# Node updates around the attention layer of a graph network: three blocks in flight, inverse roots and row loads on GpSimd

## The reference

```python
edge_index = jnp.stack([src, dst])
x = _layernorm(x + _L0_gnn_ref(x, edge_attr_3, edge_attr_64, ..., edge_index), axis=-1)
x = _layernorm(x + _L1_gnn_ref(x, edge_attr_16, edge_attr_4, ..., edge_index), axis=-1)
x = _layernorm(x + _L2_gnn_ref(x, edge_index, edge_attr_4, node_vec1, ...), axis=-1)
x = _layernorm(x + _L3_gnn_ref(x, edge_index, edge_attr_4, node_vec1, ...), axis=-1)
```

```python
# layer 0, after the sum over edges
out_s = agg_s @ W_out_s + skip_s
out_v = jnp.einsum('nmi,mk->nki', agg_v, W_out_v) + skip_v
fs = jax.nn.silu(out_s[:, :MUL0])
gate = jax.nn.sigmoid(out_s[:, MUL0:MUL0 + 32])
gv = gate[:, :, None] * out_v
# layer 1, before the edges: s_n, v_n = _equiv_layernorm(s, v, ...), then two products by node
mu = jnp.mean(s, axis=-1, keepdims=True)
var = jnp.var(s, axis=-1, keepdims=True)
s_n = (s - mu) * jax.lax.rsqrt(var + EPS) * gamma_s + beta_s
rms = jnp.sqrt(jnp.mean(jnp.sum(v * v, axis=-1), axis=-1, keepdims=True) + EPS)
v_n = v / rms[..., None] * gamma_v[None, :, None]
# layer 1, after the edges: softmax over the edges of a node, then
agg = jax.ops.segment_sum(alpha * h, dst, num_segments=n)
out = node + jnp.concatenate([agg_s @ Wps, ...], axis=-1)
# each layer norm
return (x - m) / jnp.sqrt(v + eps)
```

## Time and profile before

| | us |
|---|---|
| median of 3 runs | 26809.61 |
| lowest and highest | 26806.86, 26810.96 |
| the profiled execution | 26817.98 |
| its span, from the first instruction to the last | 26815.9 |
| n1, by its loads and stores | about 6185 to 6883 |
| n2 | about 17982 to 18533 |
| n3 and n4 | about 20930 to 22600 and 25070 to 26815 |

### The profile page before, as it was taken

The page is one execution under the profiler, slowest core; times in us unless marked ns, Lnnn a source line. Parts: engine busy times, 40 slices in busy tenths (PEclk is TensorE's granted clock), DMA queues, the critical chain, the costliest instruction groups (busy, mean ns, idle before and its releaser), DMA issues. The chain is left out here.

```text
span 26815.9 us, 474867 instructions
## 1 busy us (share of the span) xinstructions
PE 20099.6 (75%) x102170; PEld 15503.3 (58%) x102170; DVE 19989.9 (75%) x70096; ACT 11977.1 (45%) x39978; POOL 12176.7 (45%) x11987
## 2 busy tenths in 40 slices
PE   1566566664798898888988988973777787777788
PEld 1223222223677777777777777762555676555677
DVE  8333688883688888888888888876777666777666
ACT  0233344443566666666666666653333222333222
POOL 2777655551344444444444444432777101777200
PEclk6677788887788888888888888876999898999888
DMA  0566555553222222222222222222222100222200
GB/s 32 149 172 172 125 111 111 109 110 87 78 73 73 73 73 73 73 73 73 73 73 73 73 73 73 73 69 65 61 61 61 18 5 20 61 60 60 28 5 5
DMA packets 1781692, 1962.59 MB, mean 73 GB/s; under 512 B 754160, under 2 KB 1457344, under 8 KB 1780992
## 3 DMA queue, kind: packets, MB, share of 16 engines
q0 software_dynamic: 565056, 1310.16, 18.5%
q1 hardware_dynamic: 1216576, 651.75, 10.6%
HBM read 1399.54 MB, written 561.06 MB: 73 GB/s over the span
## 5 line engine op out<-in xcount | busy, mean ns | idle before, releaser
L1445 PE MATMUL e_sums<-e_feat,e_same 128*128 128x272 f32 x13824 | 3442.0, 403 | 1360.1 <-ACT e_feat L1466 1237.2
L1427 POOL DMA_INDIRECT e_rows<-x,e_take x3456 | 3618.9, 1047 | 1122.6 <-issue 1045.8
L977 POOL DMA_INDIRECT e_srow<-src_table,e_take x1620 | 1557.5, 961 | 5316.6 <-issue 5126.8
L1445 PEld LDWEIGHTS e_sums<-e_feat,e_same 128*128 128x128 f32 x13824 | 2594.4, 192 | 2207.4 <-issue 1596.4
L581 PE MATMUL e_sums<-e_feat,e_same 128*128 128x480 f32 x3456 | 1965.0, 724 | 1331.1 <-DVE e_feat L649 1331.1
L1012 PE MATMUL e_ps_m<-ident,e_m 128*128 128x128 f32 x12960 | 2333.4, 308 | 554.7 <-DVE e_m L1208 411.2
L565 POOL DMA_INDIRECT e_rows<-table,e_take x1728 | 1876.6, 1086 | 1381.0 <-issue 1351.6
L1012 PEld LDWEIGHTS e_ps_m<-ident,e_m 128*128 128x128 f32 x12960 | 1592.8, 159 | 1240.0 <-DVE e_m L1208 764.5
L581 PEld LDWEIGHTS e_sums<-e_feat,e_same 128*128 128x128 f32 x3456 | 801.9, 244 | 2494.1 <-issue 2407.6
L1026 PEld LDWEIGHTS e_ps_x<-ident,e_lg 128*128 128x128 f32 x12960 | 2188.0, 238 | 76.3
L1026 PE MATMUL e_ps_x<-ident,e_lg 128*128 128x128 f32 x12960 | 2143.5, 321 | 0.0
(11 more groups left out here) (306 smaller groups left out, 52898.4 us busy)
## 6 DMA issues: line engine op xcount, KB each, us to landing
e_pay<-pay_rows SPq DMA_DIRECT2D x432, 470.0 KB, 3.8
order_keys<-key_row SPq DMA_DIRECT2D x810, 128.0 KB
e_keys<-key_row SPq DMA_DIRECT2D x1620, 64.0 KB, 2.8
e_rows<-x,e_take POOLq DMA_INDIRECT x3456, 2.6
order_feat<-in_attr_T SPq DMA_DIRECT2D x810, 64.0 KB
comb<-n_comb SPq DMA_DIRECT2D x300, 164.0 KB, 1.9
e_rows<-table,e_take POOLq DMA_INDIRECT x1728, 4.1
pay_rows<-order_stage,order_put POOLq DMA_INDIRECT x1620
```

The source lines that it names most:

```text
L977: pool.indirect_dma_start(out=srow[t.j][:, :], out_offset=None, in_=src_table, in_offset=bass.IndirectOffsetOnAxis(ap=takes[0][t.j][:, :], ...
L1427: pool.indirect_dma_start(out=rows[t.j][:, q, :], out_offset=None, in_=x, in_offset=bass.IndirectOffsetOnAxis(ap=take[t.j][:, q:q + 1], ax ...
L1445: ins = pe.matmul(sums[b][q // G][:, 512 * h:512 * h + HALF], same[b][:, q, :], feat[b][:, q, h * HALF:(h + 1) * HALF], start=q % G == 0, ...
```

## The change

In n1 and n2 each engine now works on different blocks in one step. In n1, in step s, GpSimd loads the row and copies the sums of block s and takes the inverse roots of s-1; PE turns and multiplies s, and turns and multiplies the normalised rows of s-2; ACT copies for s and s-2; DVE does the whole of s-1; SP stores s-2. `ps_o` gets a second buffer, and the store of `new` a semaphore of its own (`kept`). The row load is issued by GpSimd's queue, behind a wait for `upd_set` of s-2.

In n2, in step s, DVE merges s-1, begins the finish of s-2, takes the exponent differences of s and then normalises s-2; PE and ACT's copy work on s-1, ACT's exponential on s. The six scalings of `runs` are one instruction over 6 x 164 columns.

In all four updates the root and the reciprocal are one instruction of GpSimd, `pow` with -0.5. The sigmoid is written as a tanh: WA and WX are halved at the start, and DVE multiplies by (tanh + 1).

```diff
-    chain.link(dve.reciprocal(stats[:, 8:9], stats[:, 8:9]))
...
-def root(act, at, squares, roots, item, nth, each):
-    act.wait_ge(squares, item.count(nth, each))
-    act.activation(at, at, ACT.Sqrt).then_inc(roots, 1)
+def inverse_root(pool, at, power, squares, roots, item, nth, each):
+    pool.wait_ge(squares, item.count(nth, each))
+    pool.tensor_tensor(at, at, power, ALU.pow).then_inc(roots, 1)
...
n1, PE:
+                def step(s):
+                    b, c = s, s.back(2)
...
+                    if c.exists():
+                        pe.wait_ge(nrm_set, c.count(1))
...
n1, ACT:
-                    act.activation(sig[b.j][:, :], ps_o[:, 0:96], ACT.Sigmoid).then_inc(sig_set, 1)
-                    root(act, stats[b.j][:, 8:9], squares, roots, b, 1, 2)
-                    root(act, stats[b.j][:, 18:20], squares, roots, b, 2, 2)
...
+                        act.activation(sig[b.j][:, :], ps_o[b.j][:, 0:96], ACT.Tanh).then_inc(sig_set, 1)
...
n1, GpSimd:
-                def step(b):
-                    if b.reuses(2):
-                        pool.wait_ge(agg_t, b.count(-1))
-                    pool.tensor_copy(agg[b.j][:, 0:AGG0], acc[:, bass.ds(b.t() * AGG0, AGG0)]).then_inc(agg_set, 1)
-                node_steps(pool, step)
+                def step(s):
+                    if s.exists():
+                        pool.wait_ge(blank, 1)
+                        if s.reuses(2):
+                            pool.wait_ge(upd_set, s.count(-1))
+                        pool.dma_start(row[s.j][:, 0:D], x[bass.ds(s.t() * P, P), :]).then_inc(row_in[s.j], 16)
+                        if s.reuses(2):
+                            pool.wait_ge(agg_t, s.count(-1))
+                        pool.tensor_copy(agg[s.j][:, 0:AGG0], acc[:, bass.ds(s.t() * AGG0, AGG0)]).then_inc(agg_set, 1)
+                    b = s.back(1)
+                    if b.exists():
+                        inverse_root(pool, stats[b.j][:, 8:9], power[:, 0:1], squares, roots, b, 1, 2)
+                        inverse_root(pool, stats[b.j][:, 18:20], power[:, 0:2], squares, roots, b, 2, 2)
+                run_steps(pool, step, 1, 2, NB, peel=2)
...
n1, DVE:
-                    dve.tensor_tensor(yb[:, 0:CS], ps_o[:, 0:CS], sig[b.j][:, 0:CS], ALU.mult)
+                    dve.scalar_tensor_tensor(out=yb[:, 0:CS], in0=sig[b.j][:, 0:CS], scalar=1.0, in1=ps_o[b.j][:, 0:CS], op0=ALU.add, op1=ALU.mult)
...
-                    dve.tensor_scalar(s[:, 18:19], s[:, 16:17], EPS, None, ALU.add)
-                    dve.tensor_scalar(s[:, 19:20], s[:, 17:18], 1.0 / CV, EPS, ALU.mult, ALU.add).then_inc(squares, 1)
+                    dve.tensor_scalar(s[:, 18:20], s[:, 16:18], EPS, None, ALU.add).then_inc(squares, 1)
...
-                    link(dve.reciprocal(s[:, 18:20], s[:, 18:20]))
...
n2, DVE:
-                    for q in range(SM_TABLES):
-                        part = r[:, q, 4:SMW].rearrange("p (h m) -> p h m", h=4)
-                        ins = dve.tensor_tensor(part, part, bcast(wt[k][:, q, :].unsqueeze(2), (P, 4, HD)), ALU.mult)
-                    link(ins)
+                    parts = r[:, :, 4:SMW].rearrange("p k (h m) -> p k h m", h=4)
+                    link(dve.tensor_tensor(parts, parts, bcast(wt[k][:, :, :].unsqueeze(3), (P, SM_TABLES, 4, HD)), ALU.mult))
...
+                    moments(dve, norm, y[k][:, :], stats[k], squares)
+                    between()
+                    normalise(dve, y[k][:, :], stats[k], new[k][:, :], roots, b, 1, 1).then_inc(new_set, 1)
...
+                def step(s):
+                    b, p = s.back(1), s.back(2)
+                    if b.exists():
+                        merge(b)
+
+                    def ahead():
+                        if s.exists():
+                            weights(s)
+                    if p.exists():
+                        finish(p, ahead)
+                    else:
+                        ahead()
+                run_steps(dve, step, 2, 2, NB, peel=2)
...
n3 and n4, ACT:
-                            if h == 5 and p.exists():
-                                root(act, stats[p.j][:, 8:9], squares, roots, p, 1, 1)
...
n3 and n4, GpSimd:
+                    p = s.back(2)
+                    if p.exists():
+                        inverse_root(pool, stats[p.j][:, 8:9], power[:, 0:1], squares, roots, p, 1, 1)
```

More of the change, by code:

```diff
@@ L687, in end, with moments @@
         assert self.k == self.each, self.k
-def layernorm(dve, chain, y, stats, out, squares, roots, item, nth, each):
+def moments(dve, chain, y, stats, squares):
     chain.link(dve.bn_stats(stats[:, 0:6], y))
@@ L756, in step @@
                 def step(b):
-                    where = bass.ds(b.t() * P, P)
-                    if b.reuses(2):
-                        sp.wait_ge(upd_set, b.count(-1))
-                    sp.dma_start(row[b.j][:, 0:D], x[where, :]).then_inc(row_in[b.j], 16)
-                    p = b.back(1)
+                    p = b.back(2)
                     if p.exists():
                         store(p)
-                node_steps(sp, step)
-                store(Tile(NB // 2 - 1, 1, 2, NB))
+                run_steps(sp, step, 2, 2, NB, peel=2)
+                for k in two:
+                    sp.wait_ge(kept[k], 16 * (NB // 2))
                 for k in two:
@@ L770, in _ @@
             def _(pe):
[L771 removed]
+                pe.wait_ge(scaled, 2)
                 pe.wait_ge(blank, 1)
[L774 to L803 removed]
@@ L857, in _, with step @@
                 ins.then_inc(blank, 1)
-                chain = Linked(dve, chained, 11)
-                def step(b):
+                chain = Linked(dve, chained, 9)
+                def step(turn):
+                    b = turn.back(1)
+                    if not b.exists():
+                        return
                     chain.start(b)
@@ L1289, in step @@
                 def step(b):
-                    where = bass.ds(b.t() * P, P)
-                    if b.reuses(2):
-                        sp.wait_ge(agg_set, b.count(-1))
-                    for k in range(SM_TABLES):
-                        sp.dma_start(runs[b.j][:, k, :], combs[k][where, D:COMB]).then_inc(runs_in[b.j], 16)
-                    if b.reuses(2):
-                        sp.wait_ge(upd_set, b.count(-1))
-                    sp.dma_start(row[b.j][:, :], x[where, :]).then_inc(row_in[b.j], 16)
-                    p = b.back(1)
+                    if b.exists():
+                        where = bass.ds(b.t() * P, P)
+                        if b.reuses(2):
+                            sp.wait_ge(agg_set, b.count(-1))
+                        for k in range(SM_TABLES):
+                            sp.dma_start(runs[b.j][:, k, :], combs[k][where, D:COMB]).then_inc(runs_in[b.j], 16)
+                        if b.reuses(2):
+                            sp.wait_ge(upd_set, b.count(-1))
+                        sp.dma_start(row[b.j][:, :], x[where, :]).then_inc(row_in[b.j], 16)
+                    p = b.back(2)
                     if p.exists():
                         store(p)
-                node_steps(sp, step)
-                store(Tile(NB // 2 - 1, 1, 2, NB))
+                run_steps(sp, step, 2, 2, NB, peel=2)
                 for k in two:
@@ L1362, in step @@
                     link(dve.reciprocal(heads[:, :, 0:1], heads[:, :, 0:1]))
+                    sums.end()
                     if b.reuses(2):
@@ L1370, in step, with finish @@
                     ins.then_inc(agg_set, 1)
+                def finish(b, between):
+                    k = b.j
+                    norm.start(b)
                     dve.wait_ge(o_set, b.count(1))
```

227 lines of the change are left out of this document (127 added, 100 removed).

## The result

The changed kernel takes 26249.49 us (median of 4 runs, 26219.32 to 26253.64) against 26810.28 for the kernel before in the same comparison (4 runs, 26806.86 to 26825.46): ratio 0.9783, 95% interval 0.9772 to 0.9795. The forecast was 26235. The profiled execution took 26248.55 us with a span of 26246.9, 569 us less than the span before.

What follows compares the result with a forecast made beforehand. Chains through the engines bound n1 and n2, PE bounds n3 and n4. -353 (n1) - 222 (n2) + 0 (n3, n4) = -575 from 26817.98 gives 26243, or 26235 us against the median; range 26165 to 26400.

Steps and rivals of the forecast that it cites:

- n1: Update n1: with three blocks in flight the slowest remaining loop sets the block, 13.71 to 6.5 us, -353 us.
- the lag: In n1, working on different blocks in one step adds no block, since first and last pass the same chain.
- DVE's queue: In n1, DVE's own work with two root trips of 0.5 us each: a loop of 5.3 us a block.
- three loops: In n1, loops of PE, DVE and the row, 5.3 to 5.7 us, delay each other: 6.5 us a block taken.
- PE's loop: In n1, PE's transposes, copies, products and L802: 5.7 us a block, or 6.9 if L802 stays at 2.5.
- The row's loop: In n1, row load through PE, ACT and DVE to the second root: 11.2 us, once in two blocks, so 5.6.
- the second rival: GpSimd held 2.6 us a turn in n1, SP's loads 1 us late in n2: 26322 us, 12%; sign: PE waits for row.
- n2: Update n2: DVE becomes the bound, sum 6.1 to 6.3; block 10.93 to 6.4 us, -222 us.
- SP's loads: In n2, a second loop of 5.4 us through SP's six loads meets DVE's need at 5.3; 1 us later costs 49.
- n3 and n4: Updates n3 and n4: DVE's wait for the root, 4.3 us a block, moves to PE's products; 0 us gained.
- `pow` was not slow (2 us): Rival: GpSimd software needs 2 us for `pow`, blocks 8.3 us in n1 and 7.7 in n2: 26387 us, 13%.
- Held rows and late loads: Rival: GpSimd held beside DVE, n1 block 7.3 us; loads 1 us late, n2 block 7.4: 26322 us, 12%.

Runs made afterwards that it cites:

- the experiment: Inverse roots moved to GpSimd in n3 and n4 alone, against the kernel before: 28031.77 us, ratio 0.9999.

## Why the prediction was right

It forecast 26235 with a sum of -575; the profiled runs differ by 569 and the medians by 561. That it is so near is in part luck: the four phases that were changed gave 548 us, 27 less than forecast, and 22 came from phases that the change does not touch. Its steps:

- **n1, right that the slowest remaining loop sets the block, 4% short in size, wrong on which loop and why.** 6.5 us a block were forecast, 6.75 measured; -353 us against -337. Of these 16 us, 12 are the block. The other 4 lie outside the loop: 2.5 ahead of the first block's copy, 11.3 us after the first load for 8.8, where PE now waits until WX is scaled too (I had put this at under 1), and 1.0 behind the last, the cost of the lag, which I had put at nothing.
- **DVE's queue, the term that was mis-sized.** I had 5.3 us and called it one loop of three; it is 6.75 and the bound. The waits for the two roots are 0.68 and 0.90 where I had 0.5 for each trip, since `pow` runs 0.56 us on one column and 0.70 on two: 5.3 + 0.58 = 5.9. The held L913 to L915 add 0.64, the jump back of the loop 5.8 / 48 = 0.12, which makes 6.6. That I chose 6.5 for three loops "that share in-order queues" gave nearly the right number for a reason that is not what happened, which is luck: DVE hardly waits for another loop at all.
- **PE's loop, too long.** L810 takes 4 instructions in 1.24 us, as forecast (1.3 for 2.50 in the earlier trace rows), and the clock rose to 0.91. But the loop of 5.7 is at most 5.3, from the run without roots, at a clock of 1.00.
- **The row's loop.** 0.59 us of issue, landing 2.2 us after it began where I took 2.6. In 23 of 48 steps PE waits for it (38.3 us in all), without passing it on. My sign for the second rival, that PE waits for the row, was thus a bad one: it came, and the rival did not hold.
- **n2.** 6.4 forecast, 6.54 measured, -222 against -215. DVE's work is 5.6 us (5.7 forecast), and the hand-offs about 0.4 as forecast. The wait for the root (0.27) and the jump back (0.25 a block) are what I had not counted; the margin over my 6.1 to 6.3 that covered most of them was meant for SP's loads. The one scaling takes 1.18, forecast 1.17; DVE is busy for 86%, forecast over 85%. SP's loads did not come late, since DVE waits for none of them.
- **n3 and n4.** Zero forecast, and no change measured in the experiment, within 0.1%; the wait did go over to the products. L699 is held there as well, by GpSimd's own copy behind the root (650 ns against 362), and 5.6 us of cover hide it.
- **The rivals.** `pow` was not slow (2 us) but stood above the 0.5 that I took. "Held rows and late loads" had the right collision and the wrong victim: I expected GpSimd held for 2.6 us beside DVE, as in the earlier trace rows, and the price on the row's loop. What happened is that DVE is held, for 0.64 us, in the loop that bounds. The Trainium skill ("SBUF — State Buffer", "Who interferes with whom") calls the port pair a lock that goes to whichever engine issues first, while the other waits. The trace agrees where L914 begins 0.08 us behind the copy and ends 0.07 behind its end. It does not where in the records L915 starts at 6360.78, the copy at 6360.98, and it is L915 that takes 0.99 instead of 0.33: by its start in the records DVE should have won. What decides between them was not settled here. An inverse root on VectorE itself was not tried.

## What to carry to other kernels

When blocks are put in flight, count for each loop how many blocks it spans, and look for the one wait in the one in-order queue that decides it: half a step's shift of one load on GpSimd cost 5.2 us a block, and a load on SP behind stores cost the whole gain. In n1 the bound was then the queue that waits only for its own round trips; shorten these, and do not start GpSimd's loads and copies where that queue resumes. A wait that goes on an engine that is not the bound only changes its name.

## What the runs showed of the hardware

- A GpSimd `pow` in fp32 on 128 partitions takes 0.55 to 0.56 us for one column and 0.70 to 0.73 for two; from DVE's variance to its next instruction that is a wait of 0.68 and 0.90 us, where ACT's square root took 0.27 ahead of a reciprocal of 0.16 in the kernel before.
- A GpSimd copy of 0.59 us lengthened VectorE's fp32 tensor_scalar and tensor_tensor that began from 0.4 us before it to 0.2 us after it: 0.36 to 1.09 us (begun 0.38 before), 0.33 to 0.99 (0.20 before), 0.26 to 0.59 (0.08 after), 0.31 to 0.46 (0.18 after, with no load on GpSimd). Each ended 0.05 to 0.2 us after the copy. The issue of a row load lengthened a tensor_scalar begun 0.15 us after it, 0.31 to 0.59, but not one begun 0.15 us before it nor the one right behind that. The shorter statistics of the second norm were not lengthened.
- Two ACT table loads a block, 1.283 us each, cost 2.57 us of a 6.60 us block where ACT's queue is part of the bounding loop.
- PE's granted clock in n1, a mean over its two levels of 1.2 and 2.4 GHz, was higher in the kernels with the short blocks: 0.83 at 7.8 us a block, 0.91 at 6.75, 0.97 at 6.06 and 1.00 at 5.31. Among the long ones there is no such order: 0.66 at 11.9, 0.68 at 13.6 with the row on SP, 0.75 at 13.7 in the kernel before. The matmuls get longer with it: L801's mean is 399 ns at 0.91 and 546 at 0.66.
- Chips differ: on three others the same kernel takes 4.5% longer, nearly all of it in `prep`, `order`, e2, e3 and e1, which gather and sort by DMA; e0 and n1 to n4 take the same within 20 us.
